# The dense units' up products as two matmuls over 64 rows each

## What is computed

```python
h = relu(x @ W1 + b1) @ W2                       # layer 0: 64 -> 128 -> 64, then a sum over edges
x = _layernorm(x + layer0(x));  x = _layernorm(x + layer1(x))   # layer 1: the sums come ahead of the weights
x = _layernorm(x + attention(x))                 # layer 2
x = _layernorm(x + mlp(concat(x, sum of edge messages)))        # layer 3: again 128 hidden
```

## Time and profile before

| | |
|---|---|
| median of 3 runs | 3667.65 us |
| span of the profiled execution | 3669.9 us |
| instructions | 49012 |
| TensorE busy | 2668.0 us, 73% |
| GpSimd busy | 2540.0 us, 69% |
| VectorE busy | 2144.0 us, 58% |
| ScalarE busy | 1448.5 us, 39% |

### The profile page before, as it was taken

How to read it: one execution, slowest core, us unless ns; L and a number is a source line. 1 busy time by engine, 2 the same in 40 slices (tenths; PEclk the granted TensorE clock), 3 DMA queues, 4 the chain that set the end, 5 groups by cost and what they waited for, 6 DMA issues and landing times.

```text
span 3669.9 us, 49012 instructions
## 1 busy us (share of the span) xinstructions
PE 2668.0 (73%) x11672; PEld 1539.5 (42%) x11672; DVE 2144.0 (58%) x4381; ACT 1448.5 (39%) x2720; POOL 2540.0 (69%) x2123
## 2 busy tenths in 40 slices
PE   4645576999999977856566888678768857666664
PEld 2322233445555466745443444344434433333332
DVE  6534455777777755655554888455579964333332
ACT  2323233656666622322222444345534433222222
POOL 7777777777777777137876777677612237777777
PEclk9877788999999988977887888799979978777777
DMA  3454444322223455434443444233335542222221
GB/s 73 89 90 89 83 77 73 67 42 51 47 48 77 80 109 109 103 73 95 95 95 77 108 103 103 72 86 85 79 99 136 133 106 63 53 53 52 49 53 28
DMA packets 614513, 293.77 MB, mean 80 GB/s; under 512 B 539030, under 2 KB 584800, under 8 KB 614267
## 3 DMA queue, kind: packets, MB, share of 16 engines
q1 hardware_dynamic: 523192, 232.31, 26.0%
q0 software_dynamic: 91200, 60.15, 11.3%
HBM read 172.85 MB, written 117.80 MB: 79 GB/s over the span
## 4 chain that ended last, share of the span: by engine, by line
POOL 58%; issue 25%; SPq 6%; DMA 5%; DVE 4%; PE 1%; POOLq 1%; ACT 0%; DVEq 0%; ACTq 0%
POOL g_row L854 18%; POOL g_row L757 11%; POOL p_row L813 7%; POOL out_rows L931 6%; POOL node_info L789 6%; POOL g_row L915 6%; SPq L594 5%; DMA l_b<-t_x 2%; DMA g_row<-t_x,g_idx 1%; POOL xs_rows L747 1%; POOL xd_rows L747 1%; DMA g_row<-t_h,g_idx 1%; POOL wide L876 1%; SPq L599 0%; DVE rT L1650 0%
## 5 line engine op out<-in xcount | busy, mean ns | idle before, releaser
L757 POOL DMA_INDIRECT g_row<-in_x,p_idx x400 | 524.7, 1312 | 168.1 <-issue 161.6
L854 POOL DMA_INDIRECT g_row<-t_x,g_idx x400 | 527.0, 1318 | 138.0 <-issue 111.5
L1242 ACT ACTIVATE hid<-pair,b_up 128x1000 f32<-128x1000 f32 x390 | 425.9, 1092 | 245.8 <-PE pair L1002 217.2
L1023 PE MATMUL bank<-hid,w_dn 128*64 128x500 f32 x780 | 414.6, 613 | 0.0
L1022 PE MATMUL bank<-hid,w_dn 128*64 128x500 f32 x780 | 414.6, 613 | 0.0
L1001 PE MATMUL pair<-xT,w_top 128*128 128x500 f32 x570 | 332.2, 668 | 1.6 <-ACT hid L1242 0.9
L1227 ACT ACTIVATE xT<-bank 128x500 f32<-128x500 f32 x285 | 166.1, 583 | 392.2 <-PE bank L947 294.6
L1002 PE MATMUL pair<-xT,w_bot 128*128 128x500 f32 x570 | 319.8, 646 | 0.0
L813 POOL DMA_INDIRECT p_row<-node_info,p_idx x200 | 263.0, 1315 | 75.9 <-issue 53.3
L915 POOL DMA_INDIRECT g_row<-t_x,g_idx x200 | 267.5, 1338 | 69.4 <-issue 54.0
L1650 DVE SCALAR_TENSOR_TENSOR rT<-bank,b_dn,xT 128x500 f32<-128x500 f32 x285 | 209.5, 735 | 168.3 <-PE bank L1023 143.4
(11 more groups left out here) (275 smaller groups left out, 5900.1 us busy)
## 6 DMA issues: line engine op xcount, KB each, us to landing
x_in<-in_x_cols SPq DMA_DIRECT2D x105, 250.0 KB
out_rows<-x_r SPq DMA_DIRECT2D x100, 250.0 KB
t_x<-x_r SPq DMA_DIRECT2D x75, 250.0 KB
l_k<-keep_row SPq DMA_DIRECT2D x150, 125.0 KB
t_x<-n_r SPq DMA_DIRECT2D x150, 125.0 KB
l_a<-t_x SPq DMA_DIRECT2D x150, 125.0 KB
t_h<-h_r SPq DMA_DIRECT2D x50, 250.0 KB
l_k<-on_row SPq DMA_DIRECT2D x50, 250.0 KB
```

The costliest lines, as they stand in the source:

```text
L757: g.indirect_dma_start(out=g_row[r][:, j * D:(j + 1) * D], out_offset=None, in_=t["x"], in_offset=bass.IndirectOffsetOnAxis(ap=p_idx[par][ ...
L854: g.indirect_dma_start(out=g_row[q][:, i * 128:i * 128 + D], out_offset=None, in_=table, in_offset=bass.IndirectOffsetOnAxis(ap=group[:, q ...
L1023: T.matmul(run.down[D:128, 0:CH], w_dn[a.stage][:, 0:D], hid[a.b2][:, 1, :], start=True, stop=True)\
L1242: A.activation(hid[a.b2][:, :, :], run.up[a.b2][:, :, 0:CH], ACT.Relu, bias=b_up[:, a.stage:a.stage + 1]).then_inc(Cn["hid"], 1)
```

## The change

Each of the two up products of a unit reads 64 partitions in place of 128: the first partitions 0 to 63 of the weights and the columns, the second partitions 64 to 127. Their targets, their order, their waits and their semaphore stay. The change holds for all units, those of the edges' source rows too; `w_top` is used whole elsewhere and is left as it is.

```diff
-                        T.matmul(run.up[a.b2][:, 0, 0:CH], w_top[a.stage][:, :], columns[:, :], start=True, stop=True)
-                        T.matmul(run.up[a.b2][:, 1, 0:CH], w_bot[a.stage][:, :], columns[:, :], start=True, stop=True)\
+                        T.matmul(run.up[a.b2][:, 0, 0:CH], w_top[a.stage][0:D, :], columns[0:D, :], start=True, stop=True)
+                        T.matmul(run.up[a.b2][:, 1, 0:CH], w_bot[a.stage][D:128, :], columns[D:128, :], start=True, stop=True)\
                          .then_inc(Cn["up"], 1)
```

## The result

The changed kernel takes 3610.04 us (median of 4 runs, 3602.42 to 3616.11) against 3667.18 (4 runs) before: the ratio is 0.9848, 95% interval 0.9824 to 0.9872, so it is about 56 us faster. 3608 was forecast.

A forecast was written before the change was run, and what follows sets the result against it. TensorE was taken to bound the main run's dense blocks. From the profiled 3669.9 us, 56 us behind level A and 3 us in G gave 3611, or 3608 us against the median; range 3592 to 3632 us, chance 0.63.

The forecast's parts named there:

- The bound: Main run's dense blocks: TensorE sets the pace, 11.1 us per block; edge blocks and the last stage gain nothing.
- The new price of the pair: A unit's two up products on TensorE: 0.99 to 1.21 us side by side, against 5.14 us per three-unit block before.
- VectorE's floor: Main run's dense blocks: VectorE needs 8.6 us busy plus 0.7 us stopped for ScalarE's roots, 9.3 us per block.
- The upper of the two floors: Main run's dense blocks: with both engines near 9.3 to 9.6, the upper is taken, 9.6 us per block.
- The main run: Its 51 dense-block intervals each save 1.5 us, so it ends 76 us earlier.
- Level A: Stage after the main run: starting 76 us earlier, it ends 76 x 4.9/6.6 = 56 us earlier.
- C and D nothing, G 3 us: Later levels: C and D gain nothing, covered by GpSimd's gathers; G gains 3 us, between ends of 0 and 10.
- The rule against the change: TensorE drains when its tiling mode changes: small price per change, now twice a unit, then four times.
- half overlap: Up pair: only the middle two records meet, 1.50 us a pair, 3643 us in all; chance 0.13.
- no difference: Up products: rows are masked but passes stay as they are, 3668 us in all; chance 0.05.
- The slower rival: Up pair: row halves do not overlap, 1.97 us a pair, 3697 us in all; chance 0.11.
- More than I take: Main run: TensorE at 8.93, VectorE at 9.3 without friction, 1.8 us saved per block, 3590 us in all; chance 0.08.

The follow-up runs named there:

- e7: Kernel before, with the last of a unit's four transposes back issued twice on TensorE: 3684.90 us, ratio 1.0068.
- e6: Kernel before, with VectorE's sum over squares taken over 32 of 64 features: 3660.47 us, ratio 0.9988.
- e2: Kernel before, with 64-row up products only in the units beside levels C, D and G, 128 rows in the main run: 3664.03 us, ratio 1.0001.
- e5: Changed kernel, with VectorE's sum over squares taken over 32 of 64 features: 3595.22 us, ratio 0.9816 to the kernel before.
- e8: Changed kernel, with a unit's transposes placed behind the up products and ScalarE's copy behind hid: 3617.45 us, ratio 0.9863 to the kernel before.
- e9: e8, with VectorE's reciprocal also moved behind the attention layer's scaling: 3622.80 us, ratio 0.9874 to the kernel before.
- e11: e8's order together with e5's shorter sum, on the changed kernel: 3592.92 us, ratio 0.9790 to the kernel before.
- e10: Kernel before, with its 128-row products, in the orders of e9: 3678.75 us, ratio 1.0018.
- e3: Changed kernel, with both up products taking rows 0 to 63, the second half left out: 3721.73 us, ratio 1.0178 to the kernel before.

## Why the prediction was right

- **The bound**: right. e7 and e6 show TensorE alone in the main run before, and e2 shows the other stages deaf to the up products, within the 6 us of its interval. The edge blocks kept their pace (593.3 and 593.1 in this pair; 593 to 607 over all traces, of either kernel).
- **The new price of the pair**, 0.99 to 1.21 us: right, but in part by luck. The pair takes 1.04, and 1.20 with the 0.49/3 = 0.16 us that it puts on its neighbours, so TensorE's floor of 9.57 (e5) is the upper of my two ends, 9.59. The terms were sized otherwise. I allowed 0.12 us for weights of 128 columns; the pair takes 0.05 more than the down pair (1.04 against 0.99, 0.52 us from record to record against 0.47), and that the weights are the reason is not shown. I allowed 0.10 for the entry; none fell on the pair and 0.16 on the groups around it. The two errors nearly cancel.
- **VectorE's floor**, 9.3 us: 0.4 too low. What it could save was read rightly: its wait for the down products falls to 2.8 us of 360, where it was 46.9. But the pace stays at 9.69 with TensorE's floor at 9.57, and at 9.74 in e8 and e9 with TensorE's at 9.3. In the changed kernel VectorE is busy 315.94 of 360 us (I had expected above nine tenths) and waits 28.9, which makes 9.28 us per block; 0.41 us more is idle time that no wait names:

```profile
DVE rs L1584 <- ACT sd L1201: 14.7, 37, 0.4
DVE rs_b L1580 <- ACT sd_b L1201: 11.4, 37, 0.3
DVE rT L1633 <- PE bank L1006: 2.8, 18, 0.2
```

```profile
1103.04 0.19 DVE L1584 RECIPROCAL rs<-sd 125x8 f32<-125x8 f32 x1
1103.36 0.69 DVE L1618 TENSOR_TENSOR x_r<-bank,rs 125x512 f32<-125x512 f32 x1
...
1109.49 0.69 DVE L1618 TENSOR_TENSOR x_r<-bank,rs 125x512 f32<-125x512 f32 x1
1110.31 0.69 DVE L1626 TENSOR_TENSOR y_r<-x_r,b_row 125x512 f32<-125x512 f32 x1
```

  In these rows VectorE stands still for 0.13 us behind rs and again behind x_r, and both times the next instruction reads what the last one wrote. Such gaps were in neither of my terms. That they are all that is missing is my reading and no run shows it; a round through ScalarE's copy can have a part.
- **The upper of the two floors**: taking it was right, but I had it as TensorE's 9.59, and the measured 9.69 is that of VectorE's side. That 9.6 and 9.69 agree rests on the two floors lying 0.12 us apart, which was luck.
- **The main run**, 51 x 1.5 = 76 us: 75.7 measured in this pair, of which 51 x 1.41 = 72 are the pace and 4 a slightly earlier start of the dense stretch; 75.5 in the means.
- **Level A**, 56 of 76 us: 61 in this pair of traces, 57 in the means, and a slope of 0.73 over the traces against my 4.9/6.6 = 0.74. The step was right: a chunk that moves under GpSimd's gathers takes 6.5 us, not 4.9. The cap of 75 us was not reached; e11 comes to 71 and waits for xd_rows there.
- **C and D nothing, G 3 us**: C and D right. G gives nothing that can be seen (e2); 3 us are within the noise, so the term is neither shown nor excluded.
- **The rule against the change**: the price per change of shape stays about 0.1 us. A block has 11 changes where it had 6 (the unit that starts from x_in has no transposes ahead of it), and they cost 0.49 us. The Trainium skill, TensorEngine Tiling (Array Packing), Key Properties, has the array drained at each change of mode; it gives no figure, and the trace agrees with it as far as such a price goes. The order of e8 has 9 changes and takes 0.3 us of the 0.49 back from TensorE, without a gain in time. The 0.49 and 0.53 us by which I priced a group ahead of halves were of two kinds of transposes, of 125 and of 128 columns, and the first of them stood behind halves itself; like with like, the group of 125 columns takes 0.43 us between full groups (e10), 0.48 or 0.49 with one halved neighbour and 0.58 with two.
- **The rivals**: half overlap and no difference are excluded by the timeline, since the bottom product starts 0.01 us after the top one. The slower rival was a real one. e3 is what it would have been: pair 1.87 us (1.97 forecast), pace 12.06 (11.9 forecast). Its 3721.73 us lie above my 3697: G pays 10 us that I had not counted, and the rest is not placed.
- **More than I take** (3590 us) failed on both engines: TensorE's floor is 9.57 us and not 8.93, and VectorE's side stands at 9.7 and not 9.3. Only with both relieved (e11) does the pace reach 9.26, the level meant there.

## What to carry to other kernels

Two f32 products that each have zeros in half of the contraction rows can be laid in the two row halves of the array. Here their operands start at partition 0 and 64 and their results go to different banks; other places were not tried. It is the running side by side that pays, not the smaller product. Before such a change look up which engine is next and how it is coupled, with its waits and gaps and not its busy time alone: here 0.67 us on average came off a pair of products, the groups around it took 0.16 back, VectorE's side held up 0.04, and 0.47 per unit arrived. Then follow the moment at which the stage ends through the next stage, since a stage that moves under another one's DMAs passes on only part. And read a gain from more than one pair of traces: two traces of the changed kernel differ by 12 us where level B begins.

## What the runs showed of the hardware

A product over 64 rows without a partner is slower than one over 128: 0.93 us against 0.84 for 500 columns, each as the second of a pair (e3). Two of them in different halves take 1.04 us together. A group of four transposes of 128 columns takes 0.63 us between a row-halved and a column-halved group and 0.53 with one halved neighbour; one of 125 columns takes 0.58, 0.48 (e9) and, between full groups, 0.43 (e10).

The mean granted clock of the whole kernel fell from 0.855 to 0.831. In level D it is 0.85 where it was 0.90, and TensorE is busy 253.73 us of 332 there where it was 265.05; none of the stages became longer by it.
